# Weight splits of the first part in other units, L1's last products in other banks, a new order on the seam, and idle products ahead of the first

## Chip, cores and metric

The kernel runs on one core of a Trainium2 chip. The metric is the time of one execution in microseconds (us); lower is better.

## What is computed

The input x has 4 batches of 1024 tokens with 512 features. Four residual layers follow each other:

```python
x = x + concat(fc2(gelu(fc1(x))), expert[tok16](gelu(fc1(x))))   # L0: 512 -> 2048 -> 384 shared + 128 of an expert
x = x + x @ W1[tok8].T + b1[tok8]                                # L1: 512 -> 512, weights of a subject
# L2: a gate from x and a causal running mean of x, four decaying traces of the gated input,
#     blended to `temporal`; gate(temporal) * gelu(x @ Wsoma); Wout; layer norm
x = x + layernorm((gelu(x @ Wsoma.T) * sigmoid(temporal @ Wtemp.T)) @ Wout.T)
x = x + x @ W3[tok16] + b3[tok16]                                # L3: 512 -> 512, weights of a category
```

## The kernel before

**Tiles and precision.** The tokens are cut into 8 tiles t = 0 to 7 of 512 tokens, two for each batch; features lie on the partitions in KC = 4 chunks of 128. Every large product is a split product: weight and input are each a rounded high part and a remainder (low part), and TensorE (PE) runs three 128x128 by 128x512 products (lines 975 to 977) for one full one. The high part is a copy on ScalarE (ACT), the low part a subtraction on VectorE (DVE, all recorded at line 1259). A block of 4 chunks is 12 products.

**First part** (L0 and L1). It runs in units u = 16t + j. In unit u PE does fc1(u), 12 products, then fc2(u-2), 12 more; in four units of each tile (j = 4 to 7) also 12 of L1 of the tile before. ACT does the gelu of fc1(u), then h_hi (line 845) once fc2(u-2) is done; DVE does h_lo. fc1(u+2) waits for h_lo(u). All engines take their instructions strictly in the order written out by hand, so an ACT or DVE instruction that waits holds all behind it.

**Split weights that are parked.** The weights of L2 and L3 come in 37 pieces of 256 KB (`PARKED`), split in the first part: a piece is loaded into one of two staging buffers, changed on DVE in some cases (`parked_made`: sum of two pieces for WG of even number, centring for OU, identity added for L3), split into `stage_hi` and `stage_lo`, and both halves are stored to DRAM by SP's queue. `stage_lo[s]` is the same memory as `stage[s]`, so load n may start only when the store of piece n-2 has landed; there is a single `stage_hi`. `PARKED_UNITS` names the units of a round of two tiles (t odd: unit j; t even: unit j + 16) in which pieces are split: 3, 4, 5, 8, 9, 10, 12, 13, 14 and 20 to 23. The expert's weights (`exp_hi`, `exp_lo`) take the same staging buffers in units 7, 11, 15 and 19, and L1's in 24 to 27. SP issues all loads and stores in one written order (`EXP_AT` and `parked_no` number it). In units 9 and 10 of each tile its predecessor's x2 is split; four stores of 512 KB (GpSimd's queue), a store of 1 MB and, after it has landed, a load of x for a coming tile (1 MB, SP's queue) go out there. `CONST_UNIT` (j = 2 of t = 1) holds small constants with two table loads on ACT.

**Seam and second part** (L2, L3). After unit 127 PE does, for tile 0: soma; then L1 of tile 7; then rounds r = 1 to 7: gate (24 products each, four of them), `te` (the temporal gate of tile r-1), `ou` (Wout), `so` (soma), `ss` (row sums of squares, 4 small fp32 products recorded as 8), `so_pair`; from r = 2 also `rb` (broadcast of 1/std), `n1`, `mo`, and L3. DVE does for each tile and chunk `scan_g`, then `traces_a` to `traces_d` (scans, drives, adds); `spikes`, `spikes_low` feed `ou`; `sum_squares` feeds `ss`; `rows_rstd` feeds `rb`; `temporal_low` feeds the next `te`. `trace_of(i, c, 0)` overwrites `temporal` and waits for all four `te` of the tile before:

```python
                if d == 0 and i:
                    on.wait_ge(s_pe["TE"], KC * i)
```

Of the kernel before, what the change touches and what calls it, by code (L numbers as in the profile page):

```python
# [12 lines left out]
P = 128  # L13
# [5 lines left out]
NT = B * HALVES  # L19
KC = DIM // P  # L20
# [21 lines left out]
def build(nc, x, tok16, tok8, small, fc1_w, fc2_w, exp_w, exp_b, l1_w, l1_b, wg, wn1, wsoma, wtemp, wout,  # L42
# [13 lines left out]
    with ctx:  # L56
# [165 lines left out]
        TAIL = HC * LAST  # L222
        CONST_UNIT = HC + 2
        L1_UNIT = 4
# [11 lines left out]

        EXP_AT = (3, 7, 11, 12)
        ROUND = 13 + 2 * KC
# [5 lines left out]
        def l1_no(b, c):  # L244
            if b == 0:
# [3 lines left out]

        PARKED = [("WG", 0), ("WG", 1), ("N1", 0), ("WG", 2), ("WG", 3), ("SO", 0), ("WG", 4), ("WG", 5), ("SO", 1),  # L250
                  ("WG", 6), ("WG", 7), ("SO", 2), ("SO", 3)]
        PARKED += [(k, c) for k in ("TE", "OU") for c in range(KC)] + [("L3", c) for c in range(B * KC)]
        PARKED_AT = {part: p for p, part in enumerate(PARKED)}
        MADE = [p for p, (k, _) in enumerate(PARKED) if k in ("WG", "OU", "L3")]
        PARKED_UNITS = (3, 4, 5, 8, 9, 10, 12, 13, 14, HC + 4, HC + 5, HC + 6, HC + 7)

        def parked_no(p):
            b, k = divmod(p, 13)
            return FIRST + ROUND * b + k + (k >= 3) + (k >= 6) + 2 * (k >= 9)

# [38 lines left out]
        def l1_bank(t, m):  # L299
            return bank[(6, 7, 6, 7 if t < LAST - 1 else 6)[m] if t < LAST else (0, 1, 4, 5)[m]]  # L300

# [52 lines left out]
        def _(eng):  # L354
# [6 lines left out]

            load_fc1(0)
            load_fc1(1)
            load_fc1(2)
# [154 lines left out]
            for b in range(1, B):  # L519
                p = 13 * (b - 1)  # L520
                for k in range(2):
                    if b > 1 and k == 1:
                        load_x(2 * b - 1)
                    load_parked(p + k)
                load_parked(p + 2)
                load_exp(b, 0)
                for k in range(3, 6):
                    load_parked(p + k)
                store_x2(2 * b - 2)
                load_exp(b, KC)  # L530
                load_parked(p + 6)
                load_parked(p + 7)
                load_x(2 * b)
                load_parked(p + 8)
                load_exp(b, 2 * KC)
                load_exp(b, 3 * KC)
                for k in range(9, 13):
                    if p + k < len(PARKED):
                        load_parked(p + k)
                for c in range(KC):  # L540
                    load_l1(b, c)
                    if c == 2:
                        store_x2(2 * b - 1)
# [126 lines left out]
        def _(eng):  # L670
# [157 lines left out]

            for c in range(KC):
                eng.dma_start(x_raw[0][:, c, :], x[0, :, c, :]).then_inc(s_x0[c], 16)  # L830
            fc1_hi(0)
# [60 lines left out]
            temporal_hi(0, 3)  # L892
            mod_of(1)
            for c in range(KC):
                x2_hi(LAST, c)
            wg_tanh(1, 0)
            for m in range(KC):
# [4 lines left out]
            wg_tanh(1, 2)  # L902
            o_of(0, 0)
            o_of(0, 1)
            wg_tanh(1, 3)
            o_of(0, 2)
            o_of(0, 3)
            soma_of(1, 0)
# [62 lines left out]
        def _(eng):  # L971
# [31 lines left out]
            def l1(t, m):  # L1003
                if t == LAST:
                    if m >= 2:
                        on.wait_ge(s_soma, m - 1)
                else:
# [39 lines left out]
            def gate(i, m):  # L1047
                if m == 0:
                    if i > 1:
                        on.wait_ge(s_soma, KC * (i - 1) + 1)  # L1050
                    elif i:
                        on.wait_ge(s_x2, KC * NT - 1)
                    else:
                        on.wait_ge(s_mod, 1)
                elif m == 1:
                    if i > 1:
                        on.wait_ge(s_mod, i + 1)
                    else:
                        on.wait_ge(s_x2, KC * NT if i else KC * LAST)
                elif m == 2:  # L1060
# [106 lines left out]
            def l3(i, m):  # L1167
# [14 lines left out]
                mm.then_inc(s_pe["L3"], 1)  # L1182

            for u in range(UNITS + 2):
                t, j = divmod(u, HC)
# [21 lines left out]
            l1(LAST, 2)  # L1207
            mo(1)
            l1(LAST, 3)
            for r in range(1, NT):  # L1210
                if r > 1:
                    n1(r)
                if r > 1:
                    rb(r - 2)
                gate(r, 0)
                if r > 1:
                    mo(r)
                else:
                    gate(r, 1)
                for m in range(KC):  # L1220
# [34 lines left out]
        def _(eng):  # L1255
# [339 lines left out]
            temporal_low(0)  # L1595
            x2_of(LAST, 2)
            x2_of(LAST, 3)
            scan_g(1, 0)
            for c in range(KC):
                x2_lo(LAST, c)  # L1600
            traces_a(1, 0)
            for m in range(KC):
                spikes(0, m)
            spikes_low(0, 0, 2)
            spikes_low(0, 2, 2)
            traces_b(1, 0)
            scan_g(1, 1)
            traces_c(1, 0)
            traces_d(1, 0)
            traces_a(1, 1)  # L1610
# [4 lines left out]
            traces_a(1, 2)  # L1615
            traces_b(1, 2)
            scan_g(1, 3)
            traces_c(1, 2)
            traces_d(1, 2)
            sum_squares(0)  # L1620
            traces_a(1, 3)
# [124 lines left out]
```

## Time and profile before

| | |
|---|---|
| runs | 1412.39, 1412.40, 1413.32 us (median 1412.4) |
| the profiled execution's own time | 1413.11 us |
| its span in the profile | 1411.1 us |
| mean granted TensorE clock | 0.988 |
| PE busy | 1369.8 us, 97% of the span |
| DVE busy | 762.2 us, 54% |
| ACT busy | 478.6 us, 34% |
| GpSimd busy | 136.2 us, 10% |

The span is the time from the first to the last recorded instruction of the profiled execution; about 2 us lie around it. PE is busy nearly all the time. The profile divides the chip's work by engine and tells, for idle time, which instruction ended it. The granted clock has two levels here, 1.2 and 2.4 GHz; a slice of time with a value below 1.00 holds some time at the lower.

### The profile page before, as it was taken

Reading aid. Unit: us, or ns where it says so; the run is one execution under the profiler, and the core shown is the slowest. Engines: PE = TensorE matmul, PEld = TensorE weight load, DVE = VectorE, ACT = ScalarE, POOL = GpSimd, SP = SyncE. Lnnn points to the kernel's source line nnn. Section 1 sums busy time; section 2 is a strip of 40 time slices with the busy share of each in tenths; the row PEclk is TensorE's granted clock in tenths of the full one; section 3 lists DMA queues with packets and bytes.
Section 4 is the critical chain, followed back from the end, with each engine's and each line's share of the span. In section 5 each row is a group of like instructions: output and inputs, shape, how many; then the busy total and the mean of one; then the engine's idle time right before and its main releaser. Section 6 shows DMA issues by size and latency. Waiting matters only on the chain.

```text
span 1411.1 us, 15375 instructions
## 1 busy us (share of the span) xinstructions
PE 1369.8 (97%) x6000; PEld 1120.5 (79%) x6000; DVE 762.2 (54%) x1067; ACT 478.6 (34%) x799; POOL 136.2 (10%) x170
## 2 busy tenths in 40 slices
PE   7999989999999999899999999699999999999988
PEld 6888878888778888788887887578787878787877
DVE  3334333322342332332221694979797979797983
ACT  4443233332342332332321222233434342424253
POOL 5000100000100000100000220012101310032000
PEclk9999999999999999999999999899999999999999
DMA  5422541502722412712223947321232123211201
GB/s 124 139 69 82 135 142 68 173 6 75 187 84 95 149 40 78 191 66 76 82 75 114 212 152 189 110 90 61 90 120 90 60 91 119 90 60 61 90 0 60
DMA packets 68376, 140.91 MB, mean 100 GB/s; under 512 B 7328, under 2 KB 19616, under 8 KB 64336
## 3 DMA queue, kind: packets, MB, share of 16 engines
q1 hardware_dynamic: 60784, 115.66, 26.7%
q0 software_dynamic: 6944, 23.23, 6.0%
q10 hardware_dynamic: 576, 1.05, 0.2%
q8 instruction: 47, 0.77, 0.2%
q14 instruction: 25, 0.20, 0.1%
HBM read 86.85 MB, written 53.05 MB: 99 GB/s over the span
## 4 chain that ended last, share of the span: by engine, by line
PE 84%; DVE 7%; DMA 6%; ACT 1%; issue 1%; POOL 0%; SPq 0%; DVEq 0%; ACTq 0%; POOLq 0%
PE bank L975 28%; PE bank L976 27%; PE bank L977 27%; DVE drive L1415 2%; DMA wout_dram<-stage_lo 1%; DMA stage<-in_exp_w 1%; DVE drive L1400 1%; DVE temporal L1425 1%; DMA wg_dram<-stage_lo 1%; DMA l3w_dram<-stage_lo 1%; DMA x_slot<-x2hl_dram 1%; DVE temporal L1415 1%; PE bank L1042 1%; PE bank L1147 0%; PE bank L1158 0%
## 5 line engine op out<-in xcount | busy, mean ns | idle before, releaser
L1259 DVE TENSOR_TENSOR h_hl<-bank,h_hl 128x512 fp32r<-128x512 f32 x128 | 88.4, 691 | 442.4 <-ACT h_hl L845 442.4
L975 PE MATMUL bank<-x_hl,wa 128*128 128x512 f32 x512 | 202.9, 396 | 20.1 <-DVE h_hl L1259 10.7
L976 PE MATMUL bank<-x_hl,wa 128*128 128x512 f32 x512 | 201.8, 394 | 0.0
L977 PE MATMUL bank<-x_hl,wa 128*128 128x512 f32 x512 | 201.5, 394 | 0.0
L975 PE MATMUL bank<-h_hl,wa 128*128 128x512 f32 x512 | 199.3, 389 | 0.0
L976 PE MATMUL bank<-h_hl,wa 128*128 128x512 f32 x512 | 199.2, 389 | 0.0
L977 PE MATMUL bank<-h_hl,wa 128*128 128x512 f32 x512 | 199.2, 389 | 0.0
L841 ACT ACTIVATE bank<-bank,small_sb 128x512 f32<-128x512 f32 x128 | 84.1, 657 | 212.3 <-PE bank L977 212.3
L845 ACT ACTIVATE h_hl<-bank 128x512 fp32r<-128x512 f32 x128 | 76.4, 597 | 213.8 <-PE bank L977 213.2
L975 PEld LDWEIGHTS bank<-x_hl,wa 128*128 128x128 f32 x512 | 97.5, 190 | 43.6 <-DVE h_hl L1259 11.7
L1400 DVE SCALAR_TENSOR_TENSOR drive<-gated,small_sb,mod_t 128x512 f32<-128x512 f32 x128 | 91.9, 739 | 44.1 <-DMA mod_t<-mod_dram 40.8
L977 PEld LDWEIGHTS bank<-x_hl,wa 128*128 128x128 f32 x512 | 97.6, 191 | 20.8
L976 PEld LDWEIGHTS bank<-x_hl,wa 128*128 128x128 f32 x512 | 97.7, 191 | 20.2
L975 PEld LDWEIGHTS bank<-h_hl,wa 128*128 128x128 f32 x512 | 96.4, 188 | 20.0
L977 PEld LDWEIGHTS bank<-h_hl,wa 128*128 128x128 f32 x512 | 96.1, 188 | 20.2
L976 PEld LDWEIGHTS bank<-h_hl,wa 128*128 128x128 f32 x512 | 96.2, 188 | 20.0
L975 PE MATMUL bank<-x_slot,wg_hl 128*128 128x512 f32 x256 | 101.1, 395 | 1.3 <-ACT mod_row L739 1.3
L976 PE MATMUL bank<-x_slot,wg_hl 128*128 128x512 f32 x256 | 99.8, 390 | 0.0
L977 PE MATMUL bank<-x_slot,wg_hl 128*128 128x512 f32 x256 | 99.4, 388 | 0.0
L627 POOL DMA_DIRECT2D x2hl_dram<-x_hl x28 | 21.1, 769 | 627.4 <-DVE x_hl L1259 627.4
L1425 DVE TENSOR_TENSOR temporal<-drive,temporal 128x512 f32<-128x512 f32 x96 | 65.9, 686 | 1.2
L1259 DVE TENSOR_TENSOR x_hl<-x_raw,x_hl 128x512 fp32r<-128x512 f32 x96 | 61.5, 683 | 0.8 <-ACT x_hl L717 0.8
(152 smaller groups left out, 2316.4 us busy)
## 6 DMA issues: line engine op xcount, KB each, us to landing
x_slot<-x2hl_dram SPq DMA_DIRECT2D x32, 513.0 KB, 4.7
x2hl_dram<-x_hl POOLq DMA_DIRECT2D x28, 512.0 KB, 10.0
stage<-in_l_w SPq DMA_DIRECT2D x32, 256.0 KB, 3.1
x_dram<-x_raw SPq DMA_DIRECT2D x8, 1024.0 KB, 5.9
xt<-x_dram SPq DMA_DIRECT2D x8, 1024.0 KB, 5.9
mod_t<-mod_dram POOLq DMA_DIRECT2D x8, 1024.0 KB, 5.3
l3w_hl<-l3w_dram SPq DMA_DIRECT2D x16, 512.0 KB, 7.7
x_raw<-in_x SPq DMA_DIRECT2D x7, 1024.0 KB, 7.3
```

What stands on the lines that cost most here:

```text
L627: eng.dma_start(x2hl_dram[t, c, :, :, 1:1 + TOK], x_hl[t % 2][:, :, c, :].bitcast(F32)).then_inc(s_hlst[c], 16)
L841: eng.activation(ps[:, :], ps[:, :], ACT.Gelu, bias=fc1_b_sb[:, j:j + 1]).then_inc(s_gelu, 1)
L845: eng.activation(h_hl[u % 2][:, 0, :], ps[:, :], ACT.Copy).then_inc(s_hhi, 1)
L975: eng.matmul(ps, w_hi, x_hi, start=first, stop=False)
L976: eng.matmul(ps, w_hi, x_lo, start=False, stop=False)
L977: return eng.matmul(ps, w_lo, x_hi, start=False, stop=final)
L1042: eng.matmul(mo_bank(i)[0:TAUS, :], wn2_sb, h1[:, :], start=True, stop=True).then_inc(s_pe["MO"], 1)
L1259: return eng.tensor_tensor(lo, raw, hi.bitcast(F32), ALU.subtract)
L1400: eng.scalar_tensor_tensor(drive[d % 2][:, :], gated[:, :], blend_sb[:, TAUS * c + d:TAUS * c + d + 1], mod_t[:, d, :], ALU.mult, ALU.mult ...
L1415: eng.tensor_tensor_scan(traced, alpha[:, 1 + d:2 + d].to_broadcast([P, TOK]), drive[d % 2][:, :], start, ALU.mult, ALU.add).then_inc(s_tr ...
L1425: eng.tensor_tensor(temporal[:, c, :], drive[d % 2][:, :], temporal[:, c, :], ALU.add).then_inc(s_add, 1)
```

## The change

- The parked pieces are split in units 2 to 6, 13 and 14 of the odd tile and 16, 17, 18, 20, 21, 22 of the round (j = 0, 1, 2, 4, 5, 6 of the even tile). The order of the pieces and SP's written order follow. SO's pieces come last of the first round. The constants move from unit 18 to unit 17.
- The four loads of x for tile 0 move from ACT's queue to SP's, behind the first fc1 piece.
- L1's four products for tile 7 write banks 0 to 3 in place of 0, 1, 4, 5; the last two wait for soma of chunks 2 and 3. The gate products 0 and 1 of tile 1, in banks 4 and 5, no longer wait for x2 of tile 7 but for soma of chunks 0 and 1; they stand ahead of and behind L1's last product.
- On ACT `wg_tanh(1, 0)` stands ahead of the four `x2_hi`; the four `o_of(0, m)` stand together ahead of `wg_tanh(1, 3)`.
- On DVE the scans and traces of tile 1, chunk 0, and `scan_g(1, 1)` stand ahead of `spikes(0, m)`; `x2_lo` of tile 7 stands behind `traces_b(1, 0)`; `sum_squares(0)` stands ahead of `scan_g(1, 3)` and `traces_c`, `traces_d` of chunk 2.
- PE runs 12 fp32 products of `ones` (128x128 by 128x128) into bank 7 ahead of the first unit. Nothing reads them.

```diff
-        CONST_UNIT = HC + 2
+        CONST_UNIT = HC + 1
-        EXP_AT = (3, 7, 11, 12)
+        EXP_AT = (5, 6, 9, 13)
-        PARKED = [("WG", 0), ("WG", 1), ("N1", 0), ("WG", 2), ("WG", 3), ("SO", 0), ("WG", 4), ("WG", 5), ("SO", 1),
-                  ("WG", 6), ("WG", 7), ("SO", 2), ("SO", 3)]
+        PARKED = [("WG", 0), ("WG", 1), ("WG", 2), ("WG", 3), ("N1", 0), ("WG", 4), ("WG", 5), ("WG", 6), ("WG", 7),
+                  ("SO", 0), ("SO", 1), ("SO", 2), ("SO", 3)]
-        PARKED_UNITS = (3, 4, 5, 8, 9, 10, 12, 13, 14, HC + 4, HC + 5, HC + 6, HC + 7)
+        PARKED_UNITS = (2, 3, 4, 5, 6, 13, 14, HC, HC + 1, HC + 2, HC + 4, HC + 5, HC + 6)
-            return FIRST + ROUND * b + k + (k >= 3) + (k >= 6) + 2 * (k >= 9)
+            return FIRST + ROUND * b + k + 2 * (k >= 5) + (k >= 7) + (k >= 10)
-            return bank[(6, 7, 6, 7 if t < LAST - 1 else 6)[m] if t < LAST else (0, 1, 4, 5)[m]]
+            return bank[(6, 7, 6, 7 if t < LAST - 1 else 6)[m] if t < LAST else m]
             load_fc1(0)
+            for c in range(KC):
+                eng.dma_start(x_raw[0][:, c, :], x[0, :, c, :]).then_inc(s_x0[c], 16)
             load_fc1(1)
...
-                for k in range(2):
-                    if b > 1 and k == 1:
-                        load_x(2 * b - 1)
+                load_parked(p)
+                if b > 1:
+                    load_x(2 * b - 1)
+                for k in range(1, 5):
                     load_parked(p + k)
-                load_parked(p + 2)
                 load_exp(b, 0)
-                for k in range(3, 6):
+                load_exp(b, KC)
+                store_x2(2 * b - 2)
+                load_parked(p + 5)
+                load_x(2 * b)
+                load_parked(p + 6)
+                load_exp(b, 2 * KC)
+                for k in range(7, 10):
                     load_parked(p + k)
...
-                load_exp(b, 2 * KC)
                 load_exp(b, 3 * KC)
-                for k in range(9, 13):
+                for k in range(10, 13):
...
                 if t == LAST:
                     if m >= 2:
-                        on.wait_ge(s_soma, m - 1)
+                        on.wait_ge(s_soma, m + 1)
...
                     elif i:
-                        on.wait_ge(s_x2, KC * NT - 1)
+                        on.wait_ge(s_soma, 1)
...
+            on.wait_ge(s_cst, 1)
+            for _ in range(12):
+                eng.matmul(bank[7][:, 0:P], ones[:, :], ones[:, :], start=True, stop=True)
...
             mo(1)
+            gate(1, 0)
             l1(LAST, 3)
+            gate(1, 1)
...
             x2_of(LAST, 2)
+            scan_g(1, 0)
             x2_of(LAST, 3)
-            scan_g(1, 0)
+            traces_a(1, 0)
+            traces_b(1, 0)
             for c in range(KC):
                 x2_lo(LAST, c)
-            traces_a(1, 0)
+            scan_g(1, 1)
+            traces_c(1, 0)
+            traces_d(1, 0)
             for m in range(KC):
                 spikes(0, m)
             spikes_low(0, 0, 2)
             spikes_low(0, 2, 2)
-            traces_b(1, 0)
-            scan_g(1, 1)
-            traces_c(1, 0)
-            traces_d(1, 0)
...
             traces_a(1, 2)
             traces_b(1, 2)
+            sum_squares(0)
             scan_g(1, 3)
             traces_c(1, 2)
             traces_d(1, 2)
-            sum_squares(0)
```

## Rows read from the trace of the kernel before

**Rows 1.** PE's waits: waited for, us in total, times, longest.

```profile
PE bank L975 <- DVE h_hl L1259: 10.7, 5, 4.3
```

**Rows 2.** ScalarE's timeline, h_hi in units 25, 57, 89, 103, 105: start, us.

```profile
157.90 0.60 ACT L845 ACTIVATE h_hl<-bank 128x512 fp32r<-128x512 f32 x1 [1.65 <-PE bank L977]
...
360.72 0.60 ACT L845 ACTIVATE h_hl<-bank 128x512 fp32r<-128x512 f32 x1 [2.12 <-PE bank L977]
...
560.32 0.60 ACT L845 ACTIVATE h_hl<-bank 128x512 fp32r<-128x512 f32 x1 [2.05 <-PE bank L977]
...
651.76 0.60 ACT L845 ACTIVATE h_hl<-bank 128x512 fp32r<-128x512 f32 x1 [2.12 <-PE bank L977]
...
665.36 0.60 ACT L845 ACTIVATE h_hl<-bank 128x512 fp32r<-128x512 f32 x1 [2.12 <-PE bank L977]
```

**Rows 3.** SP's timeline around the first stall: start, us of the issue.

```profile
162.53 0.32 SPq L385 DMA_DIRECT2D wg_dram<-stage_lo  x1
...
174.19 0.35 SPq L399 DMA_DIRECT2D stage<-in_exp_w  x1
```

**Rows 4.** The DMA view, 100 to 200 us: issues, KB, median us to landing.

```profile
stage<-in_wg SPq DMA_DIRECT2D x6, 256.0 KB, 3.0
wg_dram<-stage_lo SPq DMA_DIRECT2D x6, 256.0 KB, 2.4
```

**Rows 5.** PE's timeline, the stall at 180 us and the last slow product.

```profile
183.86 0.79 PE L975 MATMUL bank<-x_hl,wa 128*128 128x512 f32 x1 [4.30 <-DVE h_hl L1259]
...
188.72 0.51 PE L977 MATMUL bank<-x_hl,wa 128*128 128x512 f32 x1
```

**Rows 6.** The timeline of the start, all engines.

```profile
7.92 0.77 PE L975 MATMUL bank<-x_hl,wa 128*128 128x512 f32 x1 [7.92 <-DVE x_hl L1259]
...
18.33 0.63 ACT L675 ACTIVATE wa<-stage_early 128x512 fp32r<-128x512 f32 x1 [2.07 <-DMA stage_early<-in_fc_w]
...
20.17 0.69 DVE L1259 TENSOR_TENSOR h_hl<-bank,h_hl 128x512 fp32r<-128x512 f32 x1 [0.49 <-ACT h_hl L845]
...
21.64 0.39 PE L975 MATMUL bank<-x_hl,wa 128*128 128x512 f32 x1
```

**Rows 7.** The waits of SP's queue, 0 to 30 us.

```profile
SPq L366 <- DMA idx<-in_tok: 6.1, 1, 6.1
```

**Rows 8.** VectorE's timeline on the seam, in the old order.

```profile
861.09 2.47 DVE L1259 TENSOR_TENSOR x_hl<-x_raw,x_hl 128x512 fp32r<-128x512 f32 x4
...
878.11 2.36 DVE L1259 TENSOR_TENSOR spikes_lo<-soma,ts_hi 128x1024 fp32r<-128x1024 f32 x2 [0.44 <-ACT ts_hi L769]
880.39 1.28 DVE L1415 TENSOR_TENSOR_SCAN temporal<-alpha,trace_last,drive 128x512 f32<-128x512 f32 x1
...
884.00 1.28 DVE L1376 TENSOR_TENSOR_SCAN bank<-alpha,g_last,bank 128x512 f32<-128x512 f32 x1
...
889.54 0.68 DVE L1384 SCALAR_TENSOR_TENSOR gated<-bank,xt 128x512 f32<-128x512 f32 x1
...
911.94 2.28 DVE L1471 TENSOR_TENSOR sumsq<-bank,sumsq 128x512 f32<-128x512 f32 x3
...
920.00 0.88 DVE L1481 TENSOR_SCALAR diag<-ident,rstd 128x128 f32<-128x128 f32 x4
...
943.12 1.42 DVE L1400 SCALAR_TENSOR_TENSOR drive<-gated,small_sb,mod_t 128x512 f32<-128x512 f32 x2 [6.48 <-DMA mod_t<-mod_dram]
```

**Rows 9.** ScalarE's timeline, the tanh of the last te of tile 0.

```profile
876.28 0.66 ACT L763 ACTIVATE bank<-bank,small_sb 128x512 f32<-128x512 f32 x1 [2.06 <-PE bank L977]
```

**Rows 10.** PE's timeline on the seam: ss(0) and rb(0).

```profile
914.36 1.84 PE L1147 MATMUL bank<-ones,sumsq 128*128 128x1 f32 x8 [10.81 <-DVE sumsq L1471]
...
925.88 1.05 PE L1158 MATMUL bank<-diag,ones 128*128 128x128 f32 x8
```

**Rows 11.** PE's timeline: first product after two other stalls.

```profile
398.04 0.50 PE L975 MATMUL bank<-x_hl,wa 128*128 128x512 f32 x1 [1.55 <-DVE x_hl L1259]
...
1358.11 0.77 PE L975 MATMUL bank<-ts_hi,wtemp_hl 128*128 128x512 f32 x1 [2.51 <-DVE temporal_lo L1259]
```

More of the change, by code:

```diff
@@ L520, in _ @@
                 p = 13 * (b - 1)
-                for k in range(2):
-                    if b > 1 and k == 1:
-                        load_x(2 * b - 1)
+                load_parked(p)
+                if b > 1:
+                    load_x(2 * b - 1)
+                for k in range(1, 5):
                     load_parked(p + k)
-                load_parked(p + 2)
                 load_exp(b, 0)
-                for k in range(3, 6):
-                    load_parked(p + k)
[L529 to L534, printed above, removed]
-                load_exp(b, 2 * KC)
+                load_exp(b, KC)
[5 more added lines that the diff above has]
+                for k in range(7, 10):
+                    load_parked(p + k)
                 load_exp(b, 3 * KC)
-                for k in range(9, 13):
+                for k in range(10, 13):
                     if p + k < len(PARKED):
@@ L827, in y_of @@
                                ).then_inc(s_y, 1)
-            for c in range(KC):
-                eng.dma_start(x_raw[0][:, c, :], x[0, :, c, :]).then_inc(s_x0[c], 16)
             fc1_hi(0)
@@ L893, in _ @@
             mod_of(1)
+            wg_tanh(1, 0)
             for c in range(KC):
                 x2_hi(LAST, c)
-            wg_tanh(1, 0)
             for m in range(KC):
@@ L902, in _ @@
             wg_tanh(1, 2)
-            o_of(0, 0)
-            o_of(0, 1)
+            for m in range(KC):
+                o_of(0, m)
             wg_tanh(1, 3)
-            o_of(0, 2)
-            o_of(0, 3)
             soma_of(1, 0)
@@ L1057, in gate @@
                         on.wait_ge(s_mod, i + 1)
+                    elif i:
+                        on.wait_ge(s_soma, 2)
                     else:
-                        on.wait_ge(s_x2, KC * NT if i else KC * LAST)
+                        on.wait_ge(s_x2, KC * LAST)
                 elif m == 2:
@@ L1212, in _ @@
                     n1(r)
-                if r > 1:
                     rb(r - 2)
-                gate(r, 0)
-                if r > 1:
+                    gate(r, 0)
                     mo(r)
-                else:
-                    gate(r, 1)
                 for m in range(KC):
```

## The prediction

> **What bounds the kernel now.** I read the busy shares first (PE at 97%), then PE's waits, then the timelines at each wait. So PE sets the end, and the change can only give back time in which PE stands still or runs at its lower clock. The waits name three places that the change touches: the start, the h_lo waits of the first part, 10.7 us in five pieces [rows 1], and one wait of 10.81 us for the sum of squares on the seam [rows 10].
>
> Waits alone understate the loss, so I measure the first part by one event a round. From unit 103 to unit 105 lie 60 products in 13.60 us, 0.2267 us for each [rows 2]. A round of two tiles has 32 x 24 + 8 x 12 = 864 products, 195.84 us. The rounds from unit 25 to 57 and 57 to 89 took 202.82 and 199.60 us, and the half round from 89 to 105 (432 products, 97.92 us) took 105.04 [rows 2]. Lost: 6.98, 3.76 and 7.12, together 17.9 us.
>
> Where one such loss comes from: the low half of a piece was issued at 162.53 and the load that needs its buffer only at 174.19 [rows 3], though such a store's median is 2.4 us and a load's 3.0 [rows 4]. Units 9 and 10, where that piece and its neighbour are split, are those in which 5 MB of x2 and x go out. ACT stood at the expert weights behind that load, with the gelu behind it, and PE stopped for 4.30 us until 183.86 [rows 5]. Then the clock was at its lower level: 11 products took 4.86 us to 188.72 [rows 5], in place of 2.49, so 2.4 us more.
>
> **Part one of the change: units of the splits (-17.9).** No instruction is added; 37 pieces still need 37 splits. What counts is that no split lies in units 7 to 12, beside the x traffic. The expert pieces of units 7 and 11 are loaded behind splits of units 5 and 6, before the traffic. Store and load of x then stand in SP's order with one parked load between them, and all have from about unit 9 to unit 13, some 20 us, where the slow store took 11.7 us [rows 3]. So x is there for its split in unit 13, and the late x (1.55 us at 398) [rows 11] goes too. The price is denser runs of splits: units 2 to 6, then nine pieces and two of the expert in units 13 to 22. A buffer comes back after two units, 10.88 us. Its round trip is 0.7 for the low part, 2.4 and 3.0 for the DMAs [rows 4] and about 0.5 for issues, 6.6 us; some 2.1 us of making and splitting must follow, 8.7 in all, 2.2 to spare. h_lo itself may be late by 4.1 us before PE waits (h_hi starts when fc2(u-2) ends, h_lo ends 1.3 us on, and fc1(u+2) starts 5.44 after h_hi's start). Even numbers of WG need the next piece too, which comes 5.4 us later in the early run: that holds DVE and ACT in unit 4, but units 4 to 7 carry 12 more products each (8.16 us), which hides it. Unit 17 of the first round gets x1, L1's splits and the constants with two table loads: I add up the DVE and ACT work, and h_lo(18) ends near 113.0 in place of 110.2, against 114.3 where PE needs it. Bounds: 0 given back, if the runs stall as the old ones did; 17.9 at most. I take 17.9, since the traffic is what the slow rows have and the quick ones lack.
>
> **Start (-0.8).** Before, PE's first product ran at 7.92 and the clock was low until about 11.5, which costs 8 x 0.2 = 1.6 us. The 12 idle products need only `ones` (set at about 1.2 us) and fill PE's idle time; should they run past the data, their cost is bounded by rb's 8 records in 1.05 us [rows 10], so 24 of them take 3.2 at full clock and under twice that, 6.3, at the low one: over before 7.92. x behind one weight piece on SP's queue costs SP four issues more, covered by SP's wait of 6.1 us for the indices [rows 7]; fc1's pieces 1 and 2 come later by these, but are not needed before unit 0 is over. But the gain stops soon after: the load of fc1's fourth piece, issued after the indices, held ACT until 18.33 and so h_lo(1), which ended at 20.86, and fc1(3) needs it; PE was there at 21.64 [rows 6]. That load does not move, so 0.78 us is what can be had. Bounds: 0 (the single queue is slower), 2.4 (the indices land sooner as well). The Trainium skill, "TensorE: Matmul & The Clock Gate", section "What's actually happening", says that activity releases the throttle. By that rule alone the start would give 1.6; by the rows the fourth piece caps it at 0.8.
>
> **Seam (-2.5).** PE's work is the same; what moves is DVE's order. PE had no stall from L1's last products to ss(0). The last te of tile 0 ended at 876.25 [rows 9], and stays there, as only the order of equal work ahead of it changes and soma and slots are long ready. The new order has a catch: `traces_b(1, 0)` begins with `trace_of(1, 0, 0)`, which waits for all four te. So DVE's early start is stopped at once: after `traces_a(1, 0)` DVE stands until 876.3, with x2_lo, spikes and all else behind it. From there:
>
> - traces_b 3.6 (880.39 to 884.00), x2_lo 2.4, scan 1.2, traces_c and d 4.3 (885.2 to 889.54), four spikes at 0.61 (each like the gated row of 0.68), 2.4, spikes_low for two chunks 1.2 [rows 8]: the first ou may start at 891.5. Gates 2 and 3 end at 876.25 + 48 x 0.2267 = 887.1. A new stall of 4.3 us.
> - sum_squares: it ended at 914.13. DVE was busy without a gap from 880.39 to there. New start 876.3, so 4.1 earlier; x2_lo, spikes and spikes_low (2.4 + 2.4 + 2.3 = 7.1), which were hidden before it, now lie in the run; scan_g(1, 3), traces_c and d (5.5) move behind it [rows 8]. End 914.13 - 4.1 + 7.1 - 5.5 = 911.65, and ss(0) at 911.75, 2.6 before the old 914.36 [rows 10]. PE: 4.3 stall plus 2.4 at the low clock, then 4 ou and 2 so blocks end near 910.1; it waits about 1.6.
> - then so_pair and n1, 36 products, end at 911.75 + 0.8 + 8.2 = 920.75; before, 11 products of the same 36 ran slowly. But rb(0) needs diag, whose 5.5 are back in the run: old end 920.88 + 3.05 = 923.9 [rows 8]. PE waits over 2 us again, and rb ends at about 924.2, where it ended at 926.7 [rows 10]: 2.5 us gained.
> - temporal_low(1) ends near 930.6, te(1, 0) begins at 930.8 and needs the last half 1.4 us on. DVE then meets its old wait for mod_t, 6.48 us [rows 8], which swallows the 5.5 us that DVE has lost against PE. From there all keeps step.
>
> x2_lo is 18 us later, so its four stores, tile 2's xt, the L3 weights and the first slots of tile 2 behind them on SP go out from 880 on. The slots are needed at 918, the rest later: 38 us cover them, and I cost them at nothing. Without that cover n1(2) would be late by what is missing.
> Bounds of the seam: 13.2 would be the whole stall with its clock (10.8 + 2.4); the low end is below.
>
> **Sum.** 17.9 + 0.8 + 2.5 = 21.2. The profiled execution took 1413.1 (span 1411.1), 0.7 over the median of 1412.4; against the median: 1391.2, and the profiled span should be near 1390.
>
> **Rivals.**
> 1. The clock falls in rb's wait. After 1.55 us the next product took 0.50, at full clock; after 2.51 us, with another wait 4 us ahead of it, 0.77, at the low one [rows 11]. 2.3 lies between. Price 2.4 [rows 5], and the seam is worth 0: 1393.6. [...] Chance 0.25.
> 2. Some splits of the dense runs still wait, once a round, because x's traffic lasts into unit 13 or the trip is longer than 10.9 us. Price 1 to 4 us a round, three rounds: 1394 to 1403. Against it: the 2.2 + 4.1 us to spare. Chance 0.15.
> 3. The start gives 2 us more, or DVE's run on the seam is shorter than I add up: 1386 to 1389.5. Chance 0.12. The whole seam stall gone (1380.5): only if traces_b does not wait for te; chance 0.03.
> 4. Slower than before. The dense runs are the mechanism: each buffer's trip decides the next, so if trips in units 13 to 22 pass 10.9 + 4.1 = 15 us less the 2.1 of work, as the one of 11.7 + 7 us did, PE stalls for 6.7 us (4.3 + 2.4) at every second piece, five a round: 15 x 6.7 = 100 less the 21 gained, 1490. From four such stalls on it is no gain. No quiet row comes near that. Chance 0.02. No change: 0.01.
> Forecast (1390 to 1393): 0.42.
>
> **Numbers.** Range 1387 to 1397: it holds the forecast, rival 1, most of rival 3 and a third of rival 2. Differences under 0.2% (2.8 us) can't be told from none. Faster 0.96, same 0.02, slower 0.02.
>
> **What would show it.** Rounds of 195.8 us between h_hi of units 25, 57 and 89; x loaded before unit 13. On the seam: DVE idle up to te's end, then unbroken; PE waits of about 4 us at ou(0, 0) (for spikes_lo), 1.6 at ss(0), 2 at rb(0). PE's first unit at full clock, and a wait of about 1 us at fc2(0) or fc1(3). Wrong if: a wait of PE for h_lo remains in the first part; ou(0, 0) does not wait; the fourth fc1 piece lands earlier.

## The result, and the profile after

| | before | after |
|---|---|---|
| median of 4 runs each | 1412.46 us | 1387.16 us (1386.63 to 1389.34) |
| ratio | | 0.9824, 95% interval 0.9808 to 0.9839 |
| profiled execution, its span | 1413.11, 1411.1 | 1386.63, 1384.6 |
| granted clock, PE busy | 0.988, 1369.8 | 0.997, 1366.0 (99% of the span) |

The change gives 25.3 us; forecast were 21.2. The time lies just inside the range, 0.16 above its lower end, and below the likeliest case (1390 to 1393). I read the profile after in the order of the prediction: PE's waits, one event a round, then each place. First PE's waits (waited for, us in total, times, longest):

```profile
PE bank L972 <- DVE spikes_lo L1261: 5.0, 2, 4.5
PE bank L972 <- DVE temporal_lo L1261: 2.5, 1, 2.5
PE bank L1146 <- DVE sumsq L1473: 2.0, 1, 2.0
PE bank L972 <- DVE h_hl L1261: 0.8, 1, 0.8
PE bank L1157 <- DVE diag L1483: 0.5, 1, 0.5
```

The 10.7 us for h_lo [rows 1] are down to 0.8 (one wait, at fc1(2) at 13.65 us, which there was before too), the 10.81 for the sum of squares to 2.0, and a new one of 4.5 stands at ou(0, 0). ScalarE's timeline, h_hi of units 25, 57, 89 and 105:

```profile
155.47 0.60 ACT L844 ACTIVATE h_hl<-bank 128x512 fp32r<-128x512 f32 x1 [2.12 <-PE bank L974]
...
351.31 0.60 ACT L844 ACTIVATE h_hl<-bank 128x512 fp32r<-128x512 f32 x1 [2.12 <-PE bank L974]
...
547.15 0.60 ACT L844 ACTIVATE h_hl<-bank 128x512 fp32r<-128x512 f32 x1 [2.12 <-PE bank L974]
...
645.35 0.60 ACT L844 ACTIVATE h_hl<-bank 128x512 fp32r<-128x512 f32 x1 [2.39 <-PE bank L974]
```

The rounds take 195.84, 195.84 and 98.20, where they took 202.82, 199.60 and 105.04 [rows 2]: 17.6 of the 17.9 are back there, and 0.3 more by unit 120. The 2.43 between 157.90 and 155.47 is the start. SP's timeline shows how:

```profile
152.04 0.32 SPq L462 DMA_DIRECT2D x_dram<-x_raw  x1
152.41 0.43 SPq L423 DMA_DIRECT2D stage<-in_wg  x1
163.51 0.34 SPq L458 DMA_DIRECT2D x_raw<-in_x  x1
168.30 0.33 SPq L423 DMA_DIRECT2D stage<-in_wg  x1
179.85 0.33 SPq L385 DMA_DIRECT2D wg_dram<-stage_hi  x1
180.64 0.33 SPq L387 DMA_DIRECT2D wg_dram<-stage_lo  x1
182.81 0.35 SPq L401 DMA_DIRECT2D stage<-in_exp_w  x1
```

Between 152 and 179 us no split piece is stored. The first low half after the traffic goes out at 180.64 and the load that needs its buffer at 182.81: a trip of 2.17 us, where it was 11.66 [rows 3].

The start, PE's timeline, then ScalarE's, then SP's:

```profile
1.20 4.74 PE L1186 MATMUL bank<-ones 128*128 128x128 f32 x24 [1.20 <-DVE eps_sb L1512]
6.41 0.47 PE L972 MATMUL bank<-x_hl,wa 128*128 128x512 f32 x1 [0.47 <-DVE x_hl L1261]
```

```profile
3.66 0.63 ACT L676 ACTIVATE wa<-stage_early 128x512 fp32r<-128x512 f32 x1 [1.50 <-DMA stage_early<-in_fc_w]
...
15.37 0.63 ACT L676 ACTIVATE wa<-stage_early 128x512 fp32r<-128x512 f32 x1 [1.73 <-DMA stage_early<-in_fc_w]
```

```profile
10.47 0.33 SPq L376 DMA_DIRECT2D stage_early<-in_fc_w  x1
```

The first product comes 1.51 us sooner and at full clock (0.47, was 0.77 [rows 6]). The fourth fc1 piece, which the prediction took as fixed, was used at 15.37 and not at 18.33 [rows 6]: SP's wait for the indices ended 2.5 us sooner.

The seam, VectorE's timeline, then PE's:

```profile
856.05 1.28 DVE L1417 TENSOR_TENSOR_SCAN temporal<-alpha,trace_last,drive 128x512 f32<-128x512 f32 x1 [13.65 <-PE bank L974]
...
870.01 2.35 DVE L1261 TENSOR_TENSOR spikes_lo<-soma,ts_hi 128x1024 fp32r<-128x1024 f32 x2
...
889.15 2.28 DVE L1473 TENSOR_TENSOR sumsq<-bank,sumsq 128x512 f32<-128x512 f32 x3
...
902.75 0.88 DVE L1483 TENSOR_SCALAR diag<-ident,rstd 128x128 f32<-128x128 f32 x4
```

```profile
871.38 0.47 PE L972 MATMUL bank<-ts_hi,wout_hl 128*128 128x512 f32 x1 [4.46 <-DVE spikes_lo L1261]
...
891.58 1.04 PE L1146 MATMUL bank<-ones,sumsq 128*128 128x1 f32 x8 [2.00 <-DVE sumsq L1473]
892.48 0.78 PE L972 MATMUL bank<-x_slot,wsoma_hl 128*128 128x512 f32 x1
...
903.19 1.13 PE L1157 MATMUL bank<-diag,ones 128*128 128x128 f32 x8 [0.52 <-DVE diag L1483]
...
910.71 0.50 PE L972 MATMUL bank<-ts_hi,wtemp_hl 128*128 128x512 f32 x1
```

DVE stands 13.65 us at the first scan of tile 1 and starts with te's end, as forecast; then it has no gap. te(1, 0) began at 933.31 before and begins at 910.71 now: 22.60 sooner, of which 20.30 were there when te(0, 3) ended (876.28 [rows 9] against 855.98 in ScalarE's row of its tanh). The seam gave 2.3. Behind it the span shrinks by 3.9 more. The last te, in PE's timeline:

```profile
1330.33 1.13 PE L1157 MATMUL bank<-diag,ones 128*128 128x128 f32 x8
1333.97 0.47 PE L972 MATMUL bank<-ts_hi,wtemp_hl 128*128 128x512 f32 x1 [2.52 <-DVE temporal_lo L1261]
```

Before, the same wait of 2.51 ended with a product of 0.77, at the low clock [rows 11], and 1.28 us of waiting for diag stood ahead of it; both are gone. The account of the span of this one pair of profiles: 2.4 start, 17.9 rounds, 2.3 seam, 3.9 behind it, 26.5.

### The profile page after: what moved, and what is told of

It is laid out like the page before. It is cut to its first block, busy times and chain, and to the rows that moved or that the text cites. A ratio compares the mean times of both kernels' runs of the same rounds, so it can differ in the third digit from the quotient of the medians.

```text
span 1384.6 us, 15423 instructions
## 1 busy us (share of the span) xinstructions
PE 1366.0 (99%) x6024; PEld 1119.0 (81%) x6024; DVE 761.2 (55%) x1067; ACT 479.9 (35%) x799; POOL 136.2 (10%) x170
## 4 chain that ended last, share of the span: by engine, by line
PE 90%; DVE 7%; DMA 1%; issue 1%; ACT 1%; POOL 0%; SPq 0%; DVEq 0%; POOLq 0%; ACTq 0%
PE bank L972 30%; PE bank L973 29%; PE bank L974 29%; DVE drive L1417 2%; DVE drive L1402 1%; DVE temporal L1427 1%; DVE temporal L1417 1%; PE bank L1039 1%; PE bank L1157 0%; DVE spikes_lo L1261 0%; DMA x_slot<-x2hl_dram 0%; DVE bank L1378 0%; DMA mod_t<-mod_dram 0%; PE bank L1146 0%; DMA x_raw<-in_x 0%
## 5 line engine op out<-in xcount | busy, mean ns | idle before, releaser
L972 PE MATMUL bank<-x_hl,wa 128*128 128x512 f32 x512 | 199.7, 390 | 1.4 <-DVE h_hl L1261 0.8
L974 PE MATMUL bank<-x_hl,wa 128*128 128x512 f32 x512 | 199.2, 389 | 0.0
L973 PE MATMUL bank<-x_hl,wa 128*128 128x512 f32 x512 | 199.2, 389 | 0.0
L972 PEld LDWEIGHTS bank<-x_hl,wa 128*128 128x128 f32 x512 | 96.1, 188 | 23.7 <-issue 2.7
L974 PEld LDWEIGHTS bank<-x_hl,wa 128*128 128x128 f32 x512 | 96.1, 188 | 20.1
L973 PEld LDWEIGHTS bank<-x_hl,wa 128*128 128x128 f32 x512 | 96.0, 188 | 19.7
```

Source lines behind the costliest of these rows:

```text
L972: eng.matmul(ps, w_hi, x_hi, start=first, stop=False)
L973: eng.matmul(ps, w_hi, x_lo, start=False, stop=False)
L974: return eng.matmul(ps, w_lo, x_hi, start=False, stop=final)
```

## The experiments

They ran in three groups of four, each on a chip of its own. The kernel before, which took 1412.5 us for the result, takes 1422.6 on the first (one part at a time; less traffic), 1420.6 on the second (the start without one of its edits; the two seam orders) and 1422.0 on the third (the changed kernel again; the second seam order again; two splits back; small stores later). So each time is read by its ratio to the kernel before on its own chip, or by the difference to a neighbour there. Each kernel was profiled in one execution, fourteen with the two of the result. Line numbers differ by a few between kernels.

**One part at a time.** Three kernels: before with the new units alone, with the seam alone, with x on SP's queue and the idle products alone. The first, in short (with SP's written order that belongs to it):

```diff
-        EXP_AT = (3, 7, 11, 12)
+        EXP_AT = (5, 6, 9, 13)
-        PARKED_UNITS = (3, 4, 5, 8, 9, 10, 12, 13, 14, HC + 4, HC + 5, HC + 6, HC + 7)
+        PARKED_UNITS = (2, 3, 4, 5, 6, 13, 14, HC, HC + 1, HC + 2, HC + 4, HC + 5, HC + 6)
```

> The kernel before with the new units of the splits and of the constants alone. Theory (the splits beside the x traffic cost 17.9 us, and the denser runs cost nothing): 1394.5 us, rounds of 195.8 us between h_hi of units 25, 57 and 89. Rival (part of the gain comes from the other parts, for example the earlier start): a round stays above 197 us and the time is over 1397. For the end of the kernel: if the 3.7 us that the changed kernel gained behind the seam hang on its new seam, te(7, 0) waits 1.28 + 2.51 us here as before and runs at the lower clock; if they are chance of the execution, they may show here too and the time is 1391 to 1393.

> The kernel before with the seam alone (banks of L1's last products, orders of PE, ACT and DVE). Theory: waits of 4.5 us at ou(0, 0), about 2 at ss(0) and 0.5 at rb(0) in place of 10.8 at ss(0), and 2.3 us gained: 1410.1. Rival (the seam also frees the end, where the changed kernel lost its wait at the last rb and the low clock behind it): 6 us gained, 1406.4. Rival (the whole stall goes): 1399.

> The kernel before with x on SP's queue and the idle products alone. Theory after the result: the indices land 2.5 us earlier, so fc1's fourth piece no longer holds, and fc1(3) starts 2.4 us earlier: 1410.0. Rival (the term of the prediction, fourth piece unmoved): 0.8 gained, 1411.6.

Units alone: 1397.42 against 1422.63, ratio 0.9825 (0.9802 to 0.9848), -25.2 us; its rounds took 195.84 and 195.88, PE's wait for the sum of squares was still 10.8. Seam alone: 1419.12, 0.9979 (0.9968 to 0.9990), -3.5; its rounds 205.20 and 201.93, so this chip loses 9.4 and 6.1 where that of the result lost 7.0 and 3.8. Start alone: 1417.22, 0.9965 (0.9950 to 0.9981), -5.4. Together 34.1, where the whole change gives 30.5 on the third chip (below); the parts are each known to 2 or 3 us, so they add up within that, and the units are most of it. The start alone is worth 2.7 to 7.1 by its interval, more than the 0.8 forecast.

**The traffic, a first try.** Before, with the x2 stores of tile 0 (2 MB and 1 MB, beside units 9 and 10 of tile 1) cut to 64 of 512 tokens; the rest is filled in earlier with other data, which the later layers read for tile 0. In short:

```diff
-                eng.dma_start(x2_dram[t], x_raw[t % 2][:, :, :]).then_inc(s_x2st, 16)
+                n = TOK if t else CUT
+                eng.dma_start(x2_dram[t][:, :, 0:n], x_raw[t % 2][:, :, 0:n]).then_inc(s_x2st, 16)
...
-                eng.dma_start(x2hl_dram[t, c, :, :, 1:1 + TOK], x_hl[t % 2][:, :, c, :].bitcast(F32)
+                n = TOK if t else CUT
+                eng.dma_start(x2hl_dram[t, c, :, :, 1:1 + n], x_hl[t % 2][:, :, c, 0:n].bitcast(F32)
```

> The kernel before in which the stores of tile 0's x2 in units 25 and 26 and its 1 MB store write 64 of 512 tokens (the rest of these tensors is filled with values of x in tile 0's own time, so tile 0's and 1's output is not the reference's); the units of the splits are the old ones. Theory (x traffic makes the round trip of the staging buffer long): h_hi of unit 25 to 57 takes 196 to 198 us in place of 202.8, the next rounds stay at 199.6 and 105.0; about 6 us less in all. Rival (three splits in a row and an expert piece are too dense whatever else moves): 202 to 203 us stay.

1430.3, ratio 1.006 (1.0043 to 1.0078): slower, since the filling in tile 0 cost a wait of 7.1 for `wa`. But the round is read apart from that: 203.06 from h_hi of unit 24 to that of 56, 7.2 lost in place of 9.4. Taking away most of the bytes gave back 2 us; the 196 to 198 of the theory did not come. That speaks against the bytes, but does not settle it: by the code the cut stores keep their number of pieces, each now of 256 bytes, so they too are stores in small pieces (packets under 512 B from 160 to 200 us: 885, where the kernel with the seam alone has 431), and the load of 1 MB stayed. What the cut had left alone were four stores of 1 KB beside them, the last column of each chunk, 256 pieces of 4 bytes each, with a median of 13.0 us to landing in that stretch. That asks for two more kernels.

**Two splits put back beside the traffic, with and without the small stores.** The changed kernel, with the splits of units 13 and 14 back in 9 and 10 (in short; the numbering and SP's written order follow, so that the load of x moves behind the expert's load, from 163.5 to 171.1 us in the first round):

```diff
-        EXP_AT = (5, 6, 9, 13)
+        EXP_AT = (5, 8, 9, 13)
-        PARKED_UNITS = (2, 3, 4, 5, 6, 13, 14, HC, HC + 1, HC + 2, HC + 4, HC + 5, HC + 6)
+        PARKED_UNITS = (2, 3, 4, 5, 6, 9, 10, HC, HC + 1, HC + 2, HC + 4, HC + 5, HC + 6)
```

> The changed kernel with two of the thirteen splits of each round, those of units 13 and 14, put back in units 9 and 10, beside the traffic of x2 and x. All else stays dense. Theory (the traffic makes the round trip of a staging buffer long): the expert load for unit 11 is late again, PE waits for h_lo at unit 27 or 28 of each round, and each of the two whole rounds and the half one loses 4 to 9 us, 8 to 20 us in all over the changed kernel. Rival (what counted was the old distribution over units 3 to 14 and 20 to 23 as a whole, not the traffic): rounds of 195.9, and no more than 1 us over the changed kernel.

And the same, with the small stores fed from a copy that GpSimd makes, and issued in unit 15 (for the last pair of tiles behind the x2 stores); `x_hi` then waits for the copy, not for the small store (in short):

```diff
-                    eng.dma_start(x2hl_dram[t + 1, c, :, :, 0:1], x_hl[t % 2][:, :, c, TOK - 1:TOK].bitcast(F32),
-                                  allow_slow_non_contiguous=True).then_inc(s_halo[c], 16)
+                    eng.tensor_copy(halo_sb[:, 2 * c:2 * c + 2], x_hl[t % 2][:, :, c, TOK - 1]).then_inc(s_hcp[c], 1)
...
+                    eng.dma_start(x2hl_dram[t + 1, c, :, :, 0:1],
+                                  halo_sb[:, 2 * c:2 * c + 2].bitcast(F32).rearrange("p (a n) -> p a n", n=1),
```

> As the one with two splits put back, but the four small stores of 1 KB (the last column of each chunk, 256 pieces of 4 bytes each), which go out in the midst of the x2 stores, are fed from a small copy and go out in unit 15. The megabytes in units 9 and 10 stay. Theory of the small pieces: the long round trip comes from them, so the rounds come back to within 1 us of 195.9 and the time to within 2 us of the changed kernel. Theory of the bytes (4 x 512 KB of x2 beside 1 MB and 1 MB of x): nothing changes against the one with two splits put back, within 1.5 us.

Two back: 1413.49 (1411.78 to 1414.85), 0.9947 (0.9929 to 0.9965), 22.0 over the changed kernel on the same chip. Two of thirteen splits a round cost more than two thirds of the gain. Small stores later: 1396.99 (1394.65 to 1398.10), 0.9830 (0.9812 to 0.9848); 16.5 of the 22 are back. The rounds of the first (ScalarE's timeline, h_hi of units 57, 89 and 105; unit 25 stood at 155.98):

```profile
360.64 0.60 ACT L844 ACTIVATE h_hl<-bank 128x512 fp32r<-128x512 f32 x1 [2.12 <-PE bank L974]
...
564.20 0.60 ACT L844 ACTIVATE h_hl<-bank 128x512 fp32r<-128x512 f32 x1 [2.12 <-PE bank L974]
...
669.39 0.60 ACT L844 ACTIVATE h_hl<-bank 128x512 fp32r<-128x512 f32 x1 [2.39 <-PE bank L974]
```

204.66, 203.56 and 105.19, so 8.8, 7.7 and 7.0 over the rounds after the change. With the small stores later they are 197.88, 196.66 and 99.63: 2.0, 0.8 and 1.4. The chain can be followed in the first. SP's timeline:

```profile
160.60 0.32 SPq L387 DMA_DIRECT2D wg_dram<-stage_lo  x1
170.66 0.35 SPq L401 DMA_DIRECT2D stage<-in_exp_w  x1
```

ScalarE's timeline:

```profile
168.75 0.63 ACT L676 ACTIVATE stage_hi<-stage 128x512 fp32r<-128x512 f32 x1 [5.69 <-issue]
...
181.97 0.63 ACT L676 ACTIVATE wa<-stage 128x512 fp32r<-128x512 f32 x1 [11.41 <-DMA stage<-in_exp_w]
```

PE's timeline:

```profile
184.56 0.79 PE L972 MATMUL bank<-x_hl,wa 128*128 128x512 f32 x1 [6.91 <-DVE h_hl L1261]
```

A store of 256 KB takes 10 us in place of 2, so the expert's load goes out at 170.66 and ACT stands 11.41 at it; the gelu and h_hi behind it are late, PE stops for 6.91 and goes on at the low clock. The row at 168.75 shows a second hold: the single `stage_hi` waits for the store of the high half of the piece before, which by the code is what the profile here calls "issue". Now the DMA view of this kernel, 150 to 166 us (issues, KB each, median us to landing):

```profile
x2hl_dram<-x_hl POOLq DMA_DIRECT2D x4, 512.0 KB, 12.0
...
wg_dram<-stage_lo SPq DMA_DIRECT2D x1, 256.0 KB, 9.9
x2hl_dram<-x_hl POOLq DMA_DIRECT2D x4, 1.0 KB, 12.7
```

And of the kernel with the small stores later, 150 to 166, then 166 to 190 us:

```profile
x2hl_dram<-x_hl POOLq DMA_DIRECT2D x4, 512.0 KB, 9.3
...
wg_dram<-stage_lo SPq DMA_DIRECT2D x1, 256.0 KB, 8.2
```

```profile
wg_dram<-stage_lo SPq DMA_DIRECT2D x1, 256.0 KB, 7.9
...
x2hl_dram<-halo_sb POOLq DMA_DIRECT2D x4, 1.0 KB, 2.9
```

The stores of 1 KB land in 2.9 us when alone and in 12.7 in the midst of the others. With them gone from there the x2 stores land 2.7 us sooner, and the next low half, which took 13.4 in the first kernel, takes 7.9; PE's longest wait for h_lo falls from 6.9 to 1.7. So four stores of a kilobyte in 4-byte pieces do most of the harm (19.2 us of 23.5 in the rounds), though not all, as the first of the two theories would have it: 5.5 us over the changed kernel stay. The 4.3 that stay go with all that is still in these units, the large stores and the two splits; that was not taken apart. Nor was it separated whether the number of the small pieces (1024) or their size counts.

**The start.** The changed kernel with x back on ACT's queue (the two lines below stand ahead of ACT's first weight piece instead), and without the idle products:

```diff
-            for c in range(KC):
-                eng.dma_start(x_raw[0][:, c, :], x[0, :, c, :]).then_inc(s_x0[c], 16)
```

> The changed kernel with x of tile 0 loaded by ACT's queue again; the idle products stay. Theory (the x loads in a second queue delay the indices and the first weight piece): fc2's first load goes out near 13 us in place of 10.5, fc1(3) starts over 2 us later, 2 to 2.5 us more than the changed kernel, which on a chip where the kernel before takes 1412.4 is 1389.4. Rival (the idle products and the full clock made the gain): fc1(3) starts within 0.5 us of the changed kernel's.

```diff
-            for _ in range(12):
-                eng.matmul(bank[7][:, 0:P], ones[:, :], ones[:, :], start=True, stop=True)
```

> The changed kernel without the idle products. Theory: the first unit runs at the lower clock, 12 products paced partly by x, and fc1(0) ends 1.0 to 1.6 us later; the gelu, h_lo(0) and fc1(2) follow by as much: 1.0 to 1.6 us more. Rival (x's arrival and fc1's fourth piece hide it): under 0.4 us.

x on ACT: 1393.92, 0.9810 (0.9787 to 0.9833). No idle products: 1393.33, 0.9815 (0.9787 to 0.9843). The changed kernel itself, on the third chip:

> The changed kernel once more, as the control for the three that run beside it. On the chip of the earlier experiments the kernel before took 1420.6 to 1422.6 in place of 1412.4, and its two neighbours (x on ACT's queue, no idle products) stood at ratios of 0.981 and 0.9815. If those two edits are each worth something, this one must stand lower: theory of the start (idle products and x on SP's queue both count, 2.4 us together), ratio 0.978 to 0.981. Rival (neither counts): 0.981 to 0.982 and the same time as they.

1391.46 (1387.22 to 1391.76) against 1422.0, 0.9781 (0.9763 to 0.9799). The two edits may be worth some 2 us of time each, but all three intervals overlap: not shown by the times. The profiles tell more of x's queue. h_hi of unit 25 stood, in one execution each, at 159.03, 160.40 and 162.58 in the three kernels of these groups with x on ACT's queue and tile 0's traffic untouched, and between 155.98 and 159.80, mean 157.4, in the eight with x on SP's: 3.2 us sooner in the mean. Part of the scatter are waits for h_lo near 45 us, of up to 2.9, in kernels of both kinds. Two things go with the queue in every profile. With x on its queue ACT issues four loads first (1.86 us, its table load begins at 2.76 and not 0.87), and it works on the first weight piece from 5.71, not 3.66. And SP's first load behind the indices goes out at 12.55 to 13.03 with x on ACT's queue, at 10.47 to 11.37 with x on SP's. The idle products do keep the clock up: in the five kernels without them the first unit has six to twelve slow products (over 0.55 us), in the nine with them none or one. Without them the first product took 0.76 at 6.67, at the low clock, but unit 25 stood at 157.50, in the middle of the others: that fits the prediction's account, in which a later piece sets the pace, and the idle products gave no time that these runs can tell.

**The seam.** Two orders for DVE that the first reading of the new stall suggested: the spikes ahead of everything that waits for te; and, on top, the sum of squares and the row deviations ahead of one `traces_b` each.

```diff
             traces_a(1, 0)
-            traces_b(1, 0)
             for c in range(KC):
                 x2_lo(LAST, c)
             scan_g(1, 1)
-            traces_c(1, 0)
-            traces_d(1, 0)
             for m in range(KC):
                 spikes(0, m)
             spikes_low(0, 0, 2)
             spikes_low(0, 2, 2)
+            traces_b(1, 0)
+            traces_c(1, 0)
+            traces_d(1, 0)
```

> The changed kernel with another order on DVE's seam: traces_b, c and d of tile 1, chunk 0 behind the spikes (they wait for te), x2_lo and scan_g(1, 1) ahead of the spikes. Theory (traces_b's wait for the four te holds the spikes): no wait of PE at ou(0, 0), one of 3 to 5 us at ss(0), rb(0) 4 us earlier than in the changed kernel, 3 to 4.5 us less in all. Rival (DVE's sum of work sets rb wherever the wait lies): within 1 us of the changed kernel.

> As the run before, and sum_squares(0) ahead of traces_b(1, 2), rows_rstd(0) ahead of traces_b(1, 3). Theory: ss(0) with under 1 us of wait, rb(0) some 7 us and te(1, 0) some 6 us earlier than in the changed kernel: 5 to 6.5 us less than it. Rival (temporal_low(1), behind all of DVE's work, is the real limit): no more than e6_seam_order, 3 to 4.5 us.

> The kernel with the third order on the seam once more, now beside the changed kernel itself. Theory: the changed kernel stands 5 us at ou(0, 0) because the gated traces of tile 1 wait for te, ahead of the spikes; with the spikes ahead of them, and the sum of squares and the row deviations earlier, 2 to 4 us are given back, so a ratio to the changed kernel of 0.997 to 0.9985. Rival: DVE's chain up to the next wait for mod_t swallows it, the two take the same time within 1 us.

(The last text counts the changed kernel's order as one of three; its kernel is that of the second order.)

First order: 1386.23, 0.9754 (0.9729 to 0.9779). Second: 1384.67, 0.9741 (0.9716 to 0.9766), and again, beside the changed kernel, 1383.82 (1383.21 to 1385.91), 0.9736 (0.9721 to 0.9751) where the changed kernel had 0.9781. So the second order stands 38 us under before, and 7.6 under the changed kernel by the medians, 6.4 by the ratios, and the intervals of the two do not touch. In the profiles the wait at ou(0, 0) is gone (0.5 left). Counted from h_hi of unit 120, temporal_low(1) begins at 170.36 and 170.35 in the two profiles of the changed kernel, at 166.11 in the first order and at 166.12 and 166.14 in the second: DVE's run ends 4.2 us sooner in either. te(1, 0) begins at 173.16 and 173.81 in the changed kernel, at 168.90 in the first order and at 167.48 and 167.50 in the second. So PE has 4.3 to 4.9 us there by the first order and 1.4 more by the second; the times do not tell the two orders apart (1386.23 and 1384.67, the intervals overlap). The first order leaves PE 4.10 at ss(0). The second ends that and the low clock behind it, but leaves PE 1.98 at rb(0) and then, in PE's timeline of the second order (the run beside the changed kernel),

```profile
896.62 1.13 PE L1157 MATMUL bank<-diag,ones 128*128 128x128 f32 x8 [1.98 <-DVE diag L1483]
...
906.32 0.69 PE L972 MATMUL bank<-ts_hi,wtemp_hl 128*128 128x512 f32 x1 [2.12 <-DVE temporal_lo L1261]
```

DVE has the same run of work up to temporal_low(1), whatever stands first in it, and te(1, 0) needs its end: with the second order this is the limit.

## Why the prediction was right, and where not

- **Units, 17.9 forecast, 17.9 measured.** Right in place and size; alone they give back all of the rounds' loss on another chip too. The reason given was too coarse: "the traffic" is what lengthens the trip, but by the small stores in it more than by the megabytes (which are 4 by the issues of units 9 and 10, four stores of 512 KB and a store and a load of 1 MB, and not 5). The page "DMA: Bandwidth & Descriptors" of the Trainium skill, "Specifications", says that transfers below 512 bytes make the DMA engine read, modify and write; no run here shows that mechanism, only that stores in 4-byte pieces are dear amid others (the x2 stores landed in 12.0 us with them and in 9.3 without).
- **Start, 0.8 forecast, 2.4 measured: the term was mis-sized.** The step that failed is "That load does not move, so 0.78 us is what can be had". It moved: SP's wait for the indices ended 2.5 us sooner, the first load behind it going out at 10.47 in place of 13.03. The bound of 2.4, "the indices land sooner as well", was the case, and so was one of the prediction's own signs of being wrong, "the fourth fc1 piece lands earlier". It goes with the queue: all nine profiles with x on SP's queue have that load between 10.47 and 11.37, all five without between 12.55 and 13.03. Why the indices land sooner stays open. The size is known less well: the start alone gave 5.4 by the times (2.7 to 7.1), and the eight kernels with x on SP's queue of the experiments differ by 3.8 us at unit 25.
- **Seam, 2.5 forecast, 2.3 measured.** The sums shifted by 20.3: ou(0, 0) at 871.2, measured 871.38; ss(0) at 891.45, measured 891.58; diag near 903.6, measured 903.63. The waits forecast at 4.3, 1.6 and 2 were 4.46, 2.00 and 0.52. What the steps missed is that the clock fell behind the 2.00 at ss(0): eight slow products (seven of 0.63 to 0.78 and one of 0.52) took 1.7 us more than at full clock and filled most of the wait for diag, so the low clock cost nothing here. (The prediction's "11 products of the same 36 ran slowly" before is eight too, from 916.06 to 919.19 us.) In the second profile of the changed kernel thirteen were slow, and te(1, 0) came 0.65 later. Over all profiles the new seam gives 2.7 in the mean by te(1, 0): it begins 175.5 to 176.7 us behind h_hi of unit 120 in the four with the old seam and 173.1 to 173.8 in the seven with the new one. The first of the two new orders shows the price of the other stall: the one at ou(0, 0), which the prediction derived from te's wait, was worth 4.3 to 4.9.
- **Behind the seam, 3.9 not forecast.** "From there all keeps step" was wrong by this in the profiled pair. 1.3 is the wait at the last rb ahead of te(7, 0), where the last mod_t load landed 1.2 us sooner behind the same issue; 2.4 is the low clock at te(7, 0). Both differ from one execution to the next. The wait at that rb was 0.36 to 1.47 in the four profiles with the old seam and between 0 and 1.50 in the seven with the new one. The wait at te(7, 0) was 2.5 in all fourteen profiles. Slow products followed it at once in eight, and 0.3 to 1.6 us later in five, as in the second profile of the changed kernel:

```profile
1337.25 0.47 PE L972 MATMUL bank<-ts_hi,wtemp_hl 128*128 128x512 f32 x1 [2.51 <-DVE temporal_lo L1261]
...
1338.87 0.63 PE L972 MATMUL bank<-ts_hi,wtemp_hl 128*128 128x512 f32 x1
```

Only in the changed kernel's profile of the result did none follow. From te(7, 0) to the end of the span it is 50.63 us there, 52.99 in the kernel before and 52.08 to 53.59 in the other twelve, so this 2.4 is luck of the pair. Not all of the 3.9 is. From h_hi of unit 120 to the end of the span lie 652.9 to 653.7 us in the four profiles with the old seam (mean 653.3) and 647.1 to 652.0 in the seven with the new one (mean 649.3). So of the 6.2 of seam and end together about 4 go with the new seam in the mean, where 2.5 were forecast, and the seam alone gave 3.5 by the times (1.4 to 4.6 by its interval). How the new seam gains more than its 2.7 at te(1, 0) stays open.
- **Rivals.** The time lies in the third case (1386 to 1389.5), which had 0.12, for the reason that it names, a better start (1.6 more than forecast), and for one that it doesn't, the end. The clock did not fall in rb's wait (rival 1): only 0.52 was left of it. In the kernel with two splits back the wait at rb(0) was 2.23, the rival's very case, and no slow product followed. The dense runs never stalled PE (rivals 2 and 4): behind the start no wait for h_lo is left. That a long trip stalls PE, as rival 4 has it, the kernel with two splits back shows: one stall of 4.6 to 6.9 us in each of its rounds, 7.0 to 8.8 lost.

The page "TensorE: Matmul & The Clock Gate" of the Trainium skill, section "HAM oscillation — how this bites in real kernels", warns of long idle gaps. The trace agrees at ou(0, 0): 4.46 us of idling, then products of 0.63. By its length alone a gap does not tell: the clock was low after 2.00 at ss(0), 20 us behind the other, and after 2.5 at te(7, 0) in thirteen profiles, and not after the 2.52 there in the fourteenth, nor after 2.23 at rb(0) in the kernel with two splits back.

## What to carry to other kernels

Look at what a transfer is made of before you count its bytes: here four stores a round in pieces of 4 bytes, amid large ones and beside two splits, cost 16.5 us of the kernel's time, and moving them a few units later gave that back. Where a staging buffer's round trip sets a pace, keep it out of such stretches, even at the price of denser runs elsewhere. Before a block of work is moved ahead in an in-order queue, find the latest event that its first instruction waits for; everything ready that stands behind it is late too (4.2 us of DVE's time here). And before an unforecast piece of a profiled pair is explained, see how it scatters over all profiles at hand: 2.4 us here were the one execution of fourteen whose clock stayed up.

## What was not expected of the hardware

- Four stores of 1 KB in 4-byte pieces: 2.9 us to landing alone, 12.7 among x2's, whose own landing they lengthen from 9.3 to 12.0.
- The indices landed 2.5 us sooner when x went by SP's queue, although their own issue did not change; the first load behind them went out at 10.5 to 11.4 us in nine profiles, at 12.6 to 13.0 in the five with x on ACT's queue.
- The same wait of 2.5 us, at the same place, was followed by slow products in thirteen executions of fourteen, though in five of them not before 0.3 to 1.6 us had passed: the first product alone does not tell.
- Twelve idle products ahead of the first unit cut its slow products from six to twelve down to none or one.
